# Value products, V and the small products put in another order and another bank, and keys and queries of all pairs of heads split in two parts

## The reference

```python
xn = layernorm(layernorm(x)) * gamma + beta
q = xn @ w_q;  k, v = split(context @ w_kv)
attn = softmax(einsum('bqhd,bkhd->bhqk', q * SCALE, k))
out = einsum('bhqk,bkhd->bqhd', attn, v) @ w_out + b_out
x = x + tanh(g_xattn) * tanh(gate) * out
tokens = layernorm(x);  logits = tokens @ gate_w
e = argmax(softmax(logits));  pos = running count of e over all tokens
# token t goes to place pos of expert e, if pos < 160
h = relu(expert_input @ w1);  expert_output = h @ w2
x = x + tanh(g_ffn) * prob * expert_output[e, pos]
```

## Time and profile before

| | us |
|---|---|
| median of 3 runs | 475.88 |
| lowest and highest run | 473.37, 476.15 |
| span of the profiled execution | 473.7 |
| TensorE, VectorE, ScalarE, GpSimd busy | 439.7, 360.3, 386.4, 356.6 |

### The profile page before, as it was taken

The page is one execution under the profiler, slowest core; times in us unless marked ns, Lnnn a source line. Parts: engine busy times, 40 slices in busy tenths (PEclk is TensorE's granted clock), DMA queues, the critical chain, the costliest instruction groups (busy, mean ns, idle before and its releaser), DMA issues.

```text
span 473.7 us, 13155 instructions
## 1 busy us (share of the span) xinstructions
PE 439.7 (93%) x5096; PEld 334.0 (71%) x5096; DVE 360.3 (76%) x789; ACT 386.4 (82%) x630; POOL 356.6 (75%) x270
## 2 busy tenths in 40 slices
PE   7889799998999989999999999999999999988993
PEld 6656667776767767776777667776777677758892
DVE  4787687778877887779787796878877887785622
ACT  5889788899888988899888898899799998892330
POOL 3687686888788887888878877898878877871325
PEclk9999999999999999999999999999999999999998
DMA  5499999999999999999999999999989998996021
GB/s 167 150 177 192 206 187 175 170 181 204 188 176 188 210 194 180 192 192 192 198 189 197 189 196 191 185 200 209 190 157 185 193 180 147 159 182 137 14 67 46
DMA packets 283037, 82.10 MB, mean 173 GB/s; under 512 B 264387, under 2 KB 280435, under 8 KB 282976
## 3 DMA queue, kind: packets, MB, share of 16 engines
q1 hardware_dynamic: 281600, 77.96, 93.4%
q0 software_dynamic: 1376, 3.30, 2.2%
HBM read 10.83 MB, written 5.14 MB: 34 GB/s over the span
## 4 chain that ended last, share of the span: by engine, by line
PE 40%; DVE 20%; ACT 16%; DMA 10%; issue 8%; POOL 4%; POOLq 0%; SPq 0%; ACTq 0%; DVEq 0%
DVE MXL L903 9%; DMA PT<-PARTS 9%; ACT P L752 7%; DVE HL L890 4%; ACT HL L714 4%; PE psAB L1234 3%; PE psX L1319 3%; PE psAB L1241 3%; PE psO L1267 3%; ACT PARTS L762 3%; POOL PARTS L650 3%; PE psX L1355 3%; DVE VL L896 3%; PE psO L1269 3%; PE psO L1268 3%
## 5 line engine op out<-in xcount | busy, mean ns | idle before, releaser
L650 POOL TENSOR_TENSOR PARTS<-P,PARTS 128x1024 f16<-128x1024 f32 x125 | 267.4, 2145 | 63.5 <-ACT PARTS L762 61.8
L762 ACT ACTIVATE PARTS<-P 128x1024 f16<-128x1024 f32 x126 | 136.1, 1080 | 0.7
L752 ACT ACTIVATE P<-psAB,NB 128x512 f32<-128x512 f32 x128 | 81.6, 695 | 41.8 <-DVE NB L906 41.4
L903 DVE TENSOR_REDUCE MXL<-psAB 128x2 f32<-128x1024 f32 x64 | 78.4, 1224 | 41.4 <-PE psAB L1241 23.9
L1267 PE MATMUL psO<-VH,PT 128*128 128x65 f16 x1008 | 98.6, 194 | 8.3 <-DMA PT<-PARTS 7.7
L1267 PEld LDWEIGHTS psO<-VH,PT 128*128 128x128 f16 x1008 | 92.0, 98 | 12.0 <-DMA PT<-PARTS 8.9
L1268 PE MATMUL psO<-VL,PT 128*128 128x64 f16 x1008 | 98.5, 192 | 0.0
L1269 PE MATMUL psO<-VH,PT 128*128 128x65 f16 x1008 | 98.4, 193 | 0.0
L1268 PEld LDWEIGHTS psO<-VL,PT 128*128 128x128 f16 x1008 | 91.3, 98 | 0.5
L1269 PEld LDWEIGHTS psO<-VH,PT 128*128 128x128 f16 x1008 | 91.5, 97 | 0.0
L752 ACT ACTIVATE P<-psCD,NB 128x512 f32<-128x512 f32 x128 | 81.7, 703 | 0.1
(11 more groups left out here) (214 smaller groups left out, 871.7 us busy)
## 6 DMA issues: line engine op xcount, KB each, us to landing
ctx_raw<-in_ctx_dram SPq DMA_DIRECT2D x8, 256.0 KB, 3.7
w1s<-in_L_ffn_w_dram SPq DMA_DIRECT2D x8, 256.0 KB, 3.6
w2s<-in_L_ffn_w_dram SPq DMA_DIRECT2D x8, 256.0 KB, 4.0
PT<-PARTS SPq DMA_TRANSPOSE x126, 5.0
experts_table<-zeros POOLq DMA_DIRECT2D x2, 645.0 KB, 4.0
X<-in_x_dram SPq DMA_DIRECT2D x8, 128.0 KB, 4.2
wraw<-in_L_xattn_w_kv_dram SPq DMA_DIRECT2D x4, 256.0 KB, 5.3
out_dram<-row SPq DMA_DIRECT2D x8, 128.0 KB, 2.5
```

The costliest lines, as they stand in the source:

```text
L650: pool.tensor_tensor(PARTS[:, par, qt, 1], P32[:, par, qt], PARTS[:, par, qt, 0], ALU.subtract).then_inc(plo_done, 1)
L752: last = act.activation(P32[:, par, qt, SK * h:SK * h + SK], score_bank(qt)[:, SK * h:SK * h + SK], ACT.Exp, bias=NB[:, par, qt, h:h + 1])
L762: act.activation(PARTS[:, hp % 2, qt, 0], P32[:, hp % 2, qt], ACT.Copy).then_inc(phi_done[qt], 1)
L903: dve.tensor_reduce(MXL[:, par, qt, :, 0], score_bank(qt)[:].rearrange("p (h n) -> p h n", h=2), AX.X, ALU.max, negate=True).then_inc(max_ ...
```

## The change

- The small products of all batches but the last use psO, the values' bank, in place of psX. A second record, `wait_o`, keeps who may use psO next: a small product waits until the values before it are normalised, and the values wait until the small product before them has been read. In the last batch the router's products and one part of the projection stay in psX.
- On TensorE the small products now stand right behind the scores, before the keys and queries; V stands before the values in every step.
- `xt_copy` and `tokt_copy` move from ScalarE to VectorE, between the two row maxima; so do `take_ranks` (two instructions of `place`), the copy of the router's weights and all but the last instruction of `choose`.
- `v_hi` on ScalarE stands before the second `phi`.
- No pair is whole: `WHOLE` is empty, so `kq_hi`, `kq_lo` and the products of parts are done in all 64 steps.

```diff
-        WHOLE = (0, 2, 7)
+        WHOLE = ()
...
-            return psX[:, 0:SQ] if b else psO
+            return psO[:, 0:SQ]
...
                         kq_hi(*next_pair(b, hp, AHEAD))
                     if hp == CTX_STEP:
                         v_hi(*v_group(b, hp))
-                    if hp == X_STEP and not is_last(b):
-                        xt_copy(b + 1)
-                    if hp == TOKT_STEP and not is_first(b):
-                        tokt_copy(b - 1)
                     if j < LAST:
                         phi(b, hp, 0)
                     exps(b, hp, 1)
                     if ot_pair(j) >= 0:
                         ot_copy(ot_pair(j))
+                    if hp != CTX_STEP and v_group(b, hp):
+                        v_hi(*v_group(b, hp))
                     if j < LAST:
                         phi(b, hp, 1)
-                    if hp != CTX_STEP and v_group(b, hp):
-                        v_hi(*v_group(b, hp))
                     if hp == X_STEP and not is_last(b):
                         xt_hi(b + 1)
                     if hp == LOGITS_STEP and not is_first(b):
...
+            def xt_copy(b):
+                dve.wait_ge(xt_psum, b + 1)
+                dve.wait_ge(norm_scaled, 1)
+                dve.wait_ge(xt_lo_done, b)
+                dve.tensor_scalar(XS[:], x_bank(b), norm_q[:, 0:1], norm_q[:, 1:2], ALU.mult, ALU.add)\
+                   .then_inc(xt_f32, 1)
+            def tokt_copy(b):
+                dve.wait_ge(tokt_psum, b + 1)
+                dve.tensor_copy(tT[:], psO[:, 0:QT * P]).then_inc(tokt_done, 1)
...
-            def add_part(b, part, bank=psX):
+            def add_part(b, part, bank=psO):
...
                             ctxt_lo(b + 1)
                     elif j and v_group(*back(b, hp, 1)):
                         v_lo(*v_group(*back(b, hp, 1)))
-                    row_max(b, hp, 1)
+                    if hp == RANKS_STEP and b > 1:
+                        take_ranks(b - 2)
+                    if hp == X_STEP and not is_last(b):
+                        xt_copy(b + 1)
+                    if hp == TOKT_STEP and not is_first(b):
+                        tokt_copy(b - 1)
                     if hp == LOGITS_STEP and is_first(b):
                         dve.wait_ge(gw_mid_psum, 1)
                         dve.tensor_copy(gw_mid[:], ps_gw_mid).then_inc(gw_mid_done, 1)
-                    if hp == LOGITS_STEP and not is_first(b) and not is_last(b):
+                    if hp == LOGITS_STEP and not is_first(b):
                         choose(b - 1)
+                    if j == LAST:
+                        take_ranks(B - 2)
+                    row_max(b, hp, 1)
+                    if hp == LOGITS_STEP and not is_first(b):
+                        first_winner(b - 1)
                     if hp == RANKS_STEP and b > 1:
                         place(b - 2)
                     if j == LAST:
                         low_parts()
                         place(B - 2)
-                    if hp == LOGITS_STEP and is_last(b):
-                        choose(b - 1)
                     if not (is_last(b) and hp + AHEAD >= PAIRS):
                         kq_lo(*next_pair(b, hp, AHEAD))
                     if hp == CTX_STEP:
...
+            o_free = [None]
+            def wait_o(free_when):
+                if o_free[0]:
+                    pe.wait_ge(*o_free[0])
+                o_free[0] = free_when
...
                 j = b * PAIRS + hp
                 par = hp % 2
-                if j:
-                    pe.wait_ge(norm_done, turn(j) - 1)
-                else:
+                wait_o((norm_done, turn(j)))
+                if j == 0:
                     pe.wait_ge(row_consts, 1)
                 if hp % 4 == 0:
                     pe.wait_ge(v_lo_done, b * 2 * KT + KT * (hp // 4 + 1))
...
-                if bank is psX:
+            def project_part(b, pairs, bank=psO):
+
+                if bank is psO:
+                    wait_o((part_done, b + 1))
+                elif bank is psX:
                     wait_x((part_done, b + 1))
                 pe.wait_ge(ot_done, b * PAIRS + pairs[-1] + 1)
                 pe.wait_ge(wo_in, 16)
...
                 last.then_inc(proj_psum, 1)
             def project(b):
-                wait_x((x1_done, b + 1))
+                wait_o((x1_done, b + 1))
                 pe.wait_ge(ot_done, b * PAIRS + PAIRS)
                 for qt in range(QT):
-                    dst = psX[:, D * qt:D * qt + D]
+                    dst = psO[:, D * qt:D * qt + D]
                     for pair in range(PAIRS // 2, PAIRS):
                         last = pe.matmul(dst, OT[:, pair * QT + qt, :], wo[:, pair, :], start=(pair == PAIRS // 2),
                                          stop=(pair == PAIRS - 1))
...
                     if j == 1:
                         keep_busy(5, psO[:, 0:P])
                     scores(b, hp, 1)
+                    if hp == RANKS_STEP and b > 1:
+                        ranks(b - 2)
+                    if j == LAST:
+                        ranks(b - 1)
+                    if hp == PART_STEP and not is_first(b):
+                        project_part(b - 1, range(PAIRS // 2))
+                    if hp == PROJECT_STEP and not is_first(b):
+                        project(b - 1)
+                    if hp == X_STEP and not is_last(b):
+                        x_transposes(b + 1)
+                    if hp == TOKT_STEP and not is_first(b):
+                        tok_transposes(b - 1)
+                    if hp == LOGITS_STEP and is_first(b):
+                        router_weights()
+                    if hp == LOGITS_STEP and not is_first(b):
+                        logits(b - 1)
                     if ahead:
                         if is_first(b) and hp == 2:
                             pe.wait_ge(w_lo_rest_done, 3)
...
                             pe.wait_ge(kq_done, LAST + 1)
                             pe.wait_ge(ot_done, ot_pair(j))
                         o_transposes(ot_pair(j))
-                    if hp == RANKS_STEP and b > 1:
-                        ranks(b - 2)
-                    if j == LAST:
-                        ranks(b - 1)
-                    if hp == PART_STEP and not is_first(b):
-                        project_part(b - 1, range(PAIRS // 2))
-                    if hp == CTX_STEP:
+                    if v_group(b, hp):
                         v_project(*v_group(b, hp))
-                    if hp == PROJECT_STEP and not is_first(b):
-                        project(b - 1)
-                    if hp == X_STEP and not is_last(b):
-                        x_transposes(b + 1)
-                    if hp == TOKT_STEP and not is_first(b):
-                        tok_transposes(b - 1)
-                    if hp == LOGITS_STEP and is_first(b):
-                        router_weights()
-                    if hp == LOGITS_STEP and not is_first(b):
-                        logits(b - 1)
                     if VALUES_BEHIND <= j < LAST:
                         values(*back(b, hp, VALUES_BEHIND))
                     if hp == CTX_STEP and not is_last(b):
                         ctx_transposes(b + 1)
-                    if hp != CTX_STEP and v_group(b, hp):
-                        v_project(*v_group(b, hp))
                     if j == 0:
                         pe.wait_ge(v_lo_done, 2)
                         keep_busy(6, psO[:, 0:P])
```

More of the change, by code:

```diff
@@ L191, in gated_block, with ps_logits, ps_ranks @@
         psX = pb("psX", [P, 512])
-        ps_logits = psX[:, 0:QT * E]
-        ps_ranks = psX[:, 0:(QT + 1) * E]
-        ps_gw_mid = psX[:, 0:E]
+        def ps_logits(b):
+            return (psX if b == B - 1 else psO)[:, 0:QT * E]
+        def ps_ranks(b):
+            return (psX if b == B - 1 else psO)[:, 0:(QT + 1) * E]
+        ps_gw_mid = psO[:, 0:E]
         x_in = sem("x_in")
@@ L935, in add_attention @@
                     return
-                dve.scalar_tensor_tensor(out=x_of(b), in0=psX[:, 0:QT * D].rearrange("p (q d) -> p q d", q=QT),
+                dve.scalar_tensor_tensor(out=x_of(b), in0=psO[:, 0:QT * D].rearrange("p (q d) -> p q d", q=QT),
                                          scalar=gscale[:, 0:1], in1=X1[:, bass.ds(b * QT, QT), :], op0=ALU.mult,
                                          op1=ALU.add).then_inc(x1_done, 1)
-            def add_part(b, part, bank=psX):
+            def add_part(b, part, bank=psO):
                 dve.wait_ge(part_psum, part + 1)
@@ L1018, in place @@
                 dve.tensor_copy(taken[:], ranks[:, QT, :]).then_inc(route, 1)
+            def place(b):
+                n = b * ROUTE
                 dve.wait_ge(lexp_done, b + 1)
@@ L1101, in _ @@
             normalise_heads(B - 1, PAIRS - 3)
-            add_part(B - 1, B - 1)
+            add_part(B - 1, B - 1, psX)
             normalise_heads(B - 1, PAIRS - 1)
@@ L1279, in o_transposes, with tok_transposes @@
                 last.then_inc(ot_psum, pairs)
```

(24 more changed lines are left out.)

19 lines of the change are left out of this document (9 added, 10 removed).

## The result

The changed kernel takes **495.9 us** (median of 4 runs, 492.88 to 496.81), the kernel before, timed beside it, 475.98 us (4 runs, 473.37 to 476.15). The ratio is 1.0437, with a 95% interval of 1.0390 to 1.0485: slower by 4.4%. The forecast was 496 us, in a range of 486 to 505. The profiled span grew from 473.7 to 493.4 us; 493.8 was forecast.

What follows compares the result with a forecast made beforehand. TensorE's own work bounds steps 1 and 3, ScalarE steps 4 to 8. A batch: 1.34 - 0.17 + 2.1 - 0.4 = 2.87 us; seven give 20.1, span 473.7 to 493.8, put on the median 496 us, range 486 to 505.

Steps and rivals of the forecast that it cites:

- The signs named in advance: In the profile after: 14 value waits of some 1.6 us, ScalarE idle before kq_hi, steps 1 and 3 some 8.9 and 9.3 us.
- The working: Step 1 timetable from old row durations: cycle 8.89 instead of 7.55 us, TensorE standing still 1.57 us before the values.
- The sign on the clock: In the profile after, the clock stays at 2.4 GHz.
- relief without a stall: Rival: values start unhindered if transposes' end to the part sum's end is within V, 0.88 us; 464 us, chance 0.04.
- the stall only fills an old wait: Rival: TensorE's order only moves ScalarE's existing wait for a maximum; time stays at 473 to 479 us, chance 0.07.
- The clock rival: The clock falls to 1.2 GHz after each of the 14 stalls, another 3.2 us each: 541 us, chance 0.02.
- step 3: Step with project: values wait for add_attention, +1.58 us, and the next maximum is late, +0.5; together +2.1 a batch.
- step 1 with the start of step 2: Step with project_part: stall, +1.34 us a batch; step 2's maximum starts earlier after its scores, -0.17.
- steps 4 to 8: ScalarE's steps: three kq_hi gained, copies XS and tT lost; 29.31 against 29.75 us, -0.4 a batch.
- waits for DMA transposes in batches 1, 2 and 4: TensorE's transpose waits, six in the whole run, 7.7 us; longer steps give more room, but nothing was credited.
- batch 0, its waits for DMA transposes among it: The first batch, left with the tail at nothing, between -1 and +1 us.
- tail, behind the last first exponentials: End of the run, left with the first batch at nothing, between -1 and +1 us; small products keep their old banks.

Runs made afterwards that it cites:

- the first two experiments: Changed kernel with the two sums ahead of kq_lo on VectorE (e1, 477.46 us), or the two products back behind the transposes on TensorE (e2, 475.94 us).
- e5: e1 with token_moments moved from the end of step 3 to step 4, behind the second maximum: 484.88 us.
- e4: Changed kernel with xt_copy and tokt_copy back on ScalarE: 501.21 us, 1.0540.
- e3: Changed kernel with the 22 whole pairs back (steps 0, 2, 7): 489.55 us, 1.0271.
- b1: Kernel before with all pairs split and nothing else: 478.45 us, 1.0040.
- e7: e5 with the 22 whole pairs back: 478.69 us, 1.0029.
- e11: e7 with the three expert-weight loads of a batch issued one each in steps 1, 2 and 3: 477.38 us, 0.9997.
- e12: e1 with whole pairs back and expert-weight loads in steps 1 to 3, moments left at the end of step 3: 474.69 us, 0.9962.
- e1: Changed kernel with add_part and add_attention ahead of kq_lo on VectorE: 477.46 us, 0.9981.
- e2: Changed kernel with project_part and project back behind the transposes of outputs on TensorE, ahead of V, still in psO: 475.94 us, 0.9992.
- e13: e2 with whole pairs back and expert-weight loads in steps 1 to 3: 473.44 us, 0.9948.

## Why the prediction came out

**The mechanism** is the one forecast. The early product makes the keys late, the keys make `kq_lo` late, the sum stands behind `kq_lo` on an in-order engine, and the values wait for the sum. Taking away the order at either end (the first two experiments) takes away the whole loss. The signs named in advance are there: 14 waits, 1.64 us each (1.57 worked out), ScalarE idle ahead of `kq_hi`, steps 1 and 3 at 9.06 and 9.37 (8.9 and 9.3). The working let V begin 0.22 us behind the transposes' start, for which it shows no row; in the trace it is 0.14 (238.51 to 238.65), and with that the working gives 1.65. The sign on the clock holds at all 14 stalls, but not in the whole span, as told below. The rival *relief without a stall* fails on its own condition: from the transposes' end at 238.89 to the sum's end at 241.18 are 2.3 us, not under 0.88. The rival that the stall only fills an old wait fails too: ScalarE's wait ahead of the exponentials of step 2 of batch 4 stayed (1.92 us before, 1.63 after), and 1.51 us ahead of `kq_hi` was added.

**The clock rival** fell. The windows of the two stalled steps, TensorE, weight loads, VectorE, ScalarE and GpSimd busy with their counts, then the granted clock, DMA share and GB/s:

```profile
34.00:38.00 4.00, 1.62 (x10) 1.18 (x9) 3.96 (x5) 1.21 (x3) 2.93 (x3) 1.00 1.01 200
38.00:42.00 4.00, 4.00 (x56) 3.56 (x56) 2.21 (x5) 4.00 (x8) 2.13 (x1) 0.57 1.26 168
199.50:204.00 4.50, 2.85 (x57) 2.33 (x57) 1.49 (x3) 4.04 (x7) 2.90 (x2) 1.00 1.00 205
238.50:243.00 4.50, 2.86 (x57) 2.32 (x57) 1.46 (x3) 4.01 (x7) 3.41 (x4) 1.00 1.09 214
```

With stalls of 1.65 us in them the two lower windows stay at the upper level, 2.4 GHz; windows of the same length around the other twelve stalls show 1.00 too. The first two are batch 0, where TensorE was busy for 1.62 of 4 us and the clock of the next stretch was 0.57. The Trainium skill (TensorE: Matmul & The Clock Gate, A second HAM failure mode) tells of a kernel whose short idle stretches between groups of matmuls made the clock swing; by that rule the 14 stalls would have cost the clock, and this trace does not agree for stalls of this size. Three of the longer waits in e5 were followed by the lower clock, and one of 2.20 us there was not.

**The terms**, in us of the whole span (a batch's value times 7; in step 3 six batches at 2.03 and the last at 10.12 less 7.87):

| Term | forecast | measured |
|---|---|---|
| step 1 with the start of step 2 | 8.2 | 10.6 |
| step 3 | 14.7 | 14.4 |
| steps 4 to 8 | -2.8 | -2.3 |
| waits for DMA transposes in batches 1, 2 and 4 | 0 | -3.4 |
| batch 0, its waits for DMA transposes among it | 0 | -1.0 |
| tail, behind the last first exponentials | 0 | +2.4 |
| the rest (what is left of the span) | 0 | -1.0 |
| span | 20.1 | 19.7 |

Three terms were mis-sized: step 1, the waits for transposes and the tail. Their errors cancel, so it is luck that the median lies 0.1 us from the forecast; that the stalls and step 3 came out is not. The way from the span to the median rested on a wrong reading: the prediction took the 2.2 us between them for scatter and added them, but each of the four runs is 1.9 to 3.1 us longer than its own span.

- *Step 1.* In batch 4 the scores hold TensorE for 1.87 us instead of 1.59 (235.56 less 233.69), because the second bank waits for the exponentials before it; that wait is 10.3 us in the run (26 times, 4.6 before). The working had taken the scores' row from a step in which they were not held.
- *DMA, costed at nothing.* This is the largest miss. The prediction saw the 7.7 us of the earlier trace rows and that longer steps give more room, and still wrote nothing. The timeline before has three of the six waits in batch 0 (0.86, 2.53 and 0.91 us) and one each in batches 1, 2 and 4 (1.27, 1.53 and 0.59). The last three, 3.4 us, stand in batches that now have longer steps, and time put there paid them back about one for one: the usual batch grew by about 3.2 us, but six batches (1 to 6) grew only by 15.4 (311.7 to 327.1) and not by 19.3, because three long steps of the kernel before (7.48, 7.38 and 6.94) went. Batch 0 carries no product of a batch before and has no such stall. Its waits fell from 4.3 to 0.7 us as well, for a reason that is not shown, but it got only 1.0 us shorter, with the clock at 0.57 from 38 to 42 us.
- *The tail.* 49.9 us before, 52.3 after, outside the 1 us allowed for it. The tail's second group of transposes on TensorE (L1340) took 1.97 us instead of 1.09, and the window from 444 to 448 us shows a clock of 0.57. The other 1.5 us were not separated.

**Steps 4 to 8** came out at 29.41 us against 29.74, a third of a microsecond as worked out, but as a difference of two larger terms: undoing the move of the copies costs 5.3 us in all (e4), and undoing the split saves 6.3 (e3). The sign of such a net was not safe. In the kernel before the same split costs 2.6 us, not clear of noise (b1); why its price differs between the two kernels is not shown.

**What stays open** is why a kernel without the stalls, and with ScalarE's gain, stays within half a per cent of the old one. Without stalls the waits for transposes come back in some kernels (8.4, 15.0, 14.0, 15.0 and 10.1 us in e1, e5, e7, e11 and e12) and less in others (3.3 and 3.8 us in e2 and e13). Late moments go with the larger values. They are the one edit between e1 and e5, and between e12 and e11; the intervals of the second pair overlap, and e5 also lost the clock in places, so that they are the cause is not shown. The trace of e5 does show the last link: 13 of the 14 transposes that TensorE waited for were issued within 0.05 us of the end of the issue ahead of them on SP's queue, and their low part had been ready for 0.1 to 1.4 us. For the longest wait the low part ended at 373.22, the issue ahead of it at 373.54, and its own ran from 373.59 to 377.19. What these waited for last was the queue. Why an issue takes that long, and whether late low parts had pushed the queue back before, was not separated; that the loads do is not borne out.

## What to carry to other kernels

Before a product is moved ahead on an in-order engine, look up who reads its result, and what stands ahead of that reader on *its* engine: if what stands there is fed by the work that the product has just passed, the move makes the reader late, and whatever needs the bank next on the first engine stands still (the values in psO, V in psX). A stall is priced from the old trace's own rows, link by link, and here came out within 0.1 us. A wait that exists elsewhere on the same engine can be a credit in the sum when the steps ahead of it get longer (3.4 us here), and it can come back when they get shorter (in e1, e5 and e7, hardly in e2 and e13).

## What the runs showed of the hardware

- Fourteen stalls of 1.64 us left the clock at 1.00; a stretch with TensorE busy 1.62 of 4 us was followed by one at 0.57. In e5 three waits of 1.82 to 2.37 us were followed by a clock of 0.50, and one of 2.20 us by 1.00.
- A transpose by DMA is not one short issue here: six in a row take SP's queue 18.13 us before and 16.64 us in e7, of which 16.8 and 15.3 us are the issues themselves and the rest gaps between them.
- 88 more matmuls, products of parts in place of fp32, left TensorE with 5.9 us less busy time (439.7 to 433.8).
